# Six recurrent layers on one core: layer 1 made wide, weight loads placed behind gathers, the end split in halves

## What is computed

```python
def reference(r_state, r_token, L0_rec_ih, L0_rec_hh):
    state = r_state                      # 1024 x 256
    for i in range(6):
        gate = ih[i][token]              # 1024 rows of a 4000 x 256 table
        state = tanh(state + (state @ hh[i]) * gate)
    return state
```

## Time and profile before

| | us |
|---|---|
| median of 3 runs | 60.72 (60.33 to 61.02) |
| the profiled execution | 60.63 |
| its span, first to last instruction | 58.8 |
| what lies around the span | 1.83 |
| busy in the span: PE / DVE / ACT / POOL | 51.2 / 39.6 / 39.7 / 35.4 |

### The profile page before, as it was taken

The page is one execution under the profiler, slowest core; times in us unless marked ns, Lnnn a source line. Parts: engine busy times, 40 slices in busy tenths (PEclk is TensorE's granted clock), DMA queues, the critical chain, the costliest instruction groups (busy, mean ns, idle before and its releaser), DMA issues.

```text
span 58.8 us, 869 instructions
## 1 busy us (share of the span) xinstructions
PE 51.2 (87%) x280; PEld 43.9 (75%) x280; DVE 39.6 (67%) x62; ACT 39.7 (68%) x70; POOL 35.4 (60%) x34
## 2 busy tenths in 40 slices
PE   0979999992899999999999999999999999999000
PEld 0769988880868979888888988889888798889000
DVE  1318994974989495485976925999169990799700
ACT  0712899821073449989589999788997889944710
POOL 2076066677408445999963996479953898623400
PEclk9999999999999999999999999999999999999995
DMA  0698978798420000000000000000000000004472
GB/s 0 58 286 252 199 249 277 211 285 269 137 63 0 0 0 11 0 0 0 0 0 0 0 0 0 0 6 0 0 6 0 11 0 0 0 0 178 178 266 91
DMA packets 5524, 4.46 MB, mean 76 GB/s; under 512 B 2202, under 2 KB 5018, under 8 KB 5520
## 3 DMA queue, kind: packets, MB, share of 16 engines
q1 hardware_dynamic: 3312, 3.41, 18.6%
q0 software_dynamic: 1152, 0.73, 5.2%
q10 hardware_dynamic: 1056, 0.27, 2.0%
HBM read 8.92 MB, written 1.05 MB: 169 GB/s over the span
## 4 chain that ended last, share of the span: by engine, by line
PE 65%; DMA 10%; DVE 10%; issue 5%; POOL 2%; ACT 2%; ACTq 1%; DVEq 0%
PE prod L506 23%; PE turned L487 12%; PE prod L460 12%; PE prod L515 12%; DMA gate<-gates_dram,row_of 7%; PE turned L469 6%; DVE gate L368 3%; DMA tok<-token_dram 3%; POOL gate L237 2%; DVE gp L384 2%; DVE gp L437 1%; ACT s L312 1%; DVE pre L389 1%; DVE prod L441 1%; DVE pre L443 1%
## 5 line engine op out<-in xcount | busy, mean ns | idle before, releaser
L253 POOL TENSOR_TENSOR sl<-s,sh 128x512 fp32r<-128x512 f32 x12 | 15.4, 1294 | 6.0 <-ACT s L312 5.8
L506 PE MATMUL prod<-sh,wr 128*128 128x512 f32 (+1 forms) x68 | 17.9, 385 | 0.0
L460 PE MATMUL prod<-w,s 128*128 128x256 f32 x64 | 14.8, 379 | 0.0
L395 DVE TENSOR_TENSOR prod<-prod,gate_t 128x512 f32<-128x512 f32 x14 | 9.8, 700 | 6.6 <-PE prod L515 6.6
L506 PEld LDWEIGHTS prod<-sh,wr 128*128 128x128 f32 x68 | 12.1, 188 | 2.1
L460 PEld LDWEIGHTS prod<-w,s 128*128 128x128 f32 x64 | 11.8, 192 | 1.3
L237 POOL DMA_INDIRECT gate<-gates_dram,row_of x8 | 8.1, 1010 | 5.8 <-issue 2.0
L312 ACT ACTIVATE s<-pre 128x512 f32<-128x512 f32 x15 | 9.3, 623 | 1.1 <-DVE pre L400 1.1
L515 PE MATMUL prod<-sl,wr 128*128 128x512 f32 (+1 forms) x34 | 10.1, 377 | 0.0
L400 DVE TENSOR_TENSOR pre<-prod,s 128x512 f32<-128x512 f32 x14 | 9.7, 692 | 0.5
L297 ACT ACTIVATE s<-pre 128x512 f32<-128x512 f32 x8 | 5.0, 623 | 7.0 <-DVE pre L389 5.7
(11 more groups left out here) (28 smaller groups left out, 32.9 us busy)
## 6 DMA issues: line engine op xcount, KB each, us to landing
w<-hh_dram SPq DMA_DIRECT2D x5, 256.0 KB
s<-state_t_dram SPq DMA_DIRECT2D x4, 256.0 KB, 3.5
out_t_dram<-s SPq DMA_DIRECT2D x3, 256.0 KB, 2.1
w<-hh_dram ACTq DMA_DIRECT2D x1, 256.0 KB
out_t_dram<-s SPq DMA_DIRECT2D x2, 128.0 KB, 2.0
gate<-gates_dram,row_of POOLq DMA_INDIRECT x8, 3.4
last_row<-gates_dram ACTq DMA_DIRECT2D x1, 6.0 KB, 2.7
tok<-token_dram SPq DMA_DIRECT2D x1, 4.0 KB, 1.7
```

The lines of the kernel that those rows point to most:

```text
L253: nc.gpsimd.tensor_tensor(of_unit(sl[:, l % 2], h, c), of_unit(s, h, c), of_unit(sh[:, l % 2], h, c).bitcast(f32), ALU.subtract).then_inc( ...
L395: nc.vector.tensor_tensor(prod_bank[u][:, :], prod_bank[u][:, :], gate_t[:, l % 2, u], ALU.mult).then_inc(unit_gated[u], 1)
L460: last = nc.tensor.matmul(prod[q][:, t, :], of_quarter(s, q)[:, c, t * P:(t + 1) * P], w[:, l, c, :], start=c == 0, stop=c == KC - 1)
L506: nc.tensor.matmul(bank, wr[:, l, k, half, c * P:(c + 1) * P], of_unit(sh[:, (l - 1) % 2], h, k)[:, tokens], start=half == 0 and k == 0, s ...
```

## The change

- WIDE = 1: layer 1 is done in wide units too. Its products are written out in pieces: `rounded` (rounded weights x sh), `low_of_weights`, `low_of_state`; `high_product` is the first two, `low_product` the last. In layers 1 and 2 pieces of several units are interleaved. plain(3) stands behind turn(1), turn(0) in front of plain(2).
- Rounded tanh (sh) now for the quarters of layer 0; ACT's order of tanh, casts and gate copies is new. The remainders sl of quarters 0 and 1 are made by DVE (`low_state`), those of 2 and 3 by POOL.
- SP: state 2 behind state 1, state 3 behind state 2, weights 1 right after; weights 2, 3 and 4 when the gathers of tiles 3, 5 and 7 have landed; weights 5 behind weights 3.
- POOL: `low_weights` 3 to 5 spread among the low states of layers 1 to 3.
- DVE: the last fill stands behind gating(0); patches stand behind gating(1) and gating(2).
- The end: POOL's sum of unit 2 is made in two column halves, with a tanh and a store each.

```diff
-WIDE = 2
+WIDE = 1
+LOAD_BEHIND = {2: 3, 3: 5, 4: 7}
+DVE_LOW = [0, 1]
...
 @block.sync
-                sp.wait_ge(state_in[0], 16)
+                sp.wait_ge(state_in[1], 16)
                 load_state(2)
-                sp.wait_ge(w_in[0], 16)
+                sp.wait_ge(state_in[2], 16)
                 load_state(3)
-                sp.wait_ge(state_in[1], 16)
                 load_weights(1)
-                sp.wait_ge(state_in[2], 16)
-                load_weights(2)
-                sp.wait_ge(state_in[3], 16)
-                load_weights(3)
-                for l in range(4, LAYERS):
-                    sp.wait_ge(w_in[l - 3], 16)
+                for l, t in LOAD_BEHIND.items():
+                    sp.wait_ge(gate_in[t], 16)
                     load_weights(l)
+                sp.wait_ge(w_in[3], 16)
+                load_weights(5)
...
+                sp.wait_ge(unit_s[UNITS - 2], wide_done(LAYERS - 1))
+                store(UNITS - 2, slice(0, QB))
                 sp.wait_ge(unit_s[UNITS - 1], wide_done(LAYERS - 1))
                 store(UNITS - 1, slice(0, QB))
-                sp.wait_ge(unit_s[UNITS - 2], wide_done(LAYERS - 1))
-                store(UNITS - 2, slice(0, HB))
+                sp.wait_ge(late_s, 1)
+                store(UNITS - 2, slice(QB, HB))
...
 @block.gpsimd
-                for l in range(WIDE, LAYERS - 1):
-                    low_weights(l)
-                low_state(0)
-                low_state(1)
-                low_weights(LAYERS - 1)
-                low_state(2)
-                low_state(3)
+                low_weights(1)
+                low_weights(2)
+                for q in range(QUARTERS):
+                    if q not in DVE_LOW:
+                        low_state(q)
                 for l in range(WIDE, LAYERS - 1):
                     for h in range(HALVES):
                         for c in range(KC):
                             wide_low_state(l, h, c)
+                        if (l, h) == (1, 0):
+                            low_weights(3)
+                    if 4 <= l + 2 < LAYERS:
+                        low_weights(l + 2)
...
-                nc.gpsimd.tensor_tensor(of_unit(pre, 1, 0), gated_end, of_unit(s, 1, 0), ALU.add).then_inc(unit_pre[u], 1)
+                nc.gpsimd.tensor_tensor(late_half(pre, 0), gated_end[:, 0:QB], late_half(s, 0), ALU.add).then_inc(unit_pre[u], 1)
+                nc.gpsimd.tensor_tensor(late_half(pre, 1), gated_end[:, QB:HB], late_half(s, 1), ALU.add).then_inc(late_pre, 1)
...
 @block.scalar
+                tanh_rounded(0)
+                tanh(0)
+                round_weights(1)
+                copy_gates(1, 0, 0)
+                tanh_rounded(1)
+                tanh(1)
+                round_weights(2)
+                copy_gates(1, 0, 1)
+                tanh_rounded(2)
+                tanh(2)
+                copy_gates(1, 1, 0)
+                tanh_rounded(3)
+                tanh(3)
+                copy_gates(1, 1, 1)
+                round_weights(3)
+                wide_tanh(1, 0, 0)
+                wide_tanh(1, 0, 1)
+                copy_gates(2, 0, 0)
+                copy_gates(2, 0, 1)
+                wide_tanh(1, 1, 0)
+                wide_tanh(1, 1, 1)
+                copy_gates(2, 1, 0)
+                copy_gates(2, 1, 1)
+                round_weights(4)
+                round_weights(5)
+                for l in range(2, LAYERS - 1):
...
 @block.vector
+                def low_state(q):
+                    dve.wait_ge(s_ready[q], WIDE)
+                    nc.vector.tensor_tensor(of_quarter(sl[:, (WIDE - 1) % 2], q), of_quarter(s, q),
+                                            of_quarter(sh[:, (WIDE - 1) % 2], q).bitcast(f32), ALU.subtract).then_inc(sl_ready[q], 1)
...
                 patch(0, 0, 1)
+                patch(0, 1, 1)
+                gating(0)
                 for i, t, count in DVE_FILLS[3:]:
                     fill(i, t, count)
-                patch(0, 1, 1)
-                gating(0)
-                patch(1, 0, len(EARLY_TILES))
                 sum_up(0)
                 gating(1)
-                patch(2, 0, len(EARLY_TILES))
+                patch(1, 0, len(EARLY_TILES))
                 sum_up(1)
                 gating(2)
-                gating(4)
+                patch(2, 0, len(EARLY_TILES))
+                low_state(0)
                 sum_up(2)
+                low_state(1)
                 gating(3)
-                sum_up(4)
                 sum_up(3)
...
 @block.tensor
                 plain(0)
                 plain(1)
+                turn(0)
                 plain(2)
+                turn_gates(1, 0, 0)
...
                 turn(1)
+                plain(3)
+                turn_gates(1, 0, 1)
+                turn_gates(2, 0, 0)
...
                 turn(2)
+                rounded(1, 0, 0, prod_bank[0][:, :], slice(0, HB))
+                rounded(1, 0, 1, prod_bank[1][:, :], slice(0, HB))
+                low_of_weights(1, 0, 0, prod_bank[0][:, :], slice(0, HB))
+                low_of_weights(1, 0, 1, prod_bank[1][:, :], slice(0, HB))
+                turn_gates(1, 1, 0)
...
                 turn(3)
+                low_product(1, 0, 0)
+                low_product(1, 0, 1)
+                turn_gates(1, 1, 1)
+                turn_gates(2, 0, 1)
+                high_product(1, 1, 0)
+                high_product(1, 1, 1)
+                low_product(1, 1, 0)
+                low_product(1, 1, 1)
+                turn_gates(2, 1, 0)
+                turn_gates(2, 1, 1)
+                wide_product(2, 0, 0)
+                wide_product(2, 0, 1)
+                high_product(2, 1, 0)
+                high_product(2, 1, 1)
+                low_product(2, 1, 0)
+                low_product(2, 1, 1)
+                for l in range(3, LAYERS - 1):
```

More of the change, by code:

```diff
@@ L290, in round_weights, with tanh_rounded, tanh @@
                     nc.scalar.copy(wr[:, l, :, 0], w[:, l]).then_inc(wh_ready, 1)
[L292 to L296, removed]
+                def tanh_rounded(q):
+                    act.wait_ge(pre_ready[q], WIDE)
+                    nc.scalar.activation(of_quarter(sh[:, (WIDE - 1) % 2], q), of_quarter(pre, q), ACT.Tanh).then_inc(sh_ready[q], 1)
+                def tanh(q):
+                    act.wait_ge(pre_ready[q], WIDE)
                     nc.scalar.activation(of_quarter(s, q), of_quarter(pre, q), ACT.Tanh).then_inc(s_ready[q], 1)
@@ L474, in turn_gates @@
                     u = h * KC + c
-                    pe.wait_ge(gated[2 * h], 1)
-                    pe.wait_ge(gated[2 * h + 1], 1)
+                    if l == WIDE:
+                        for t in range(h * TPH, (h + 1) * TPH):
+                            if t not in EARLY_TILES:
+                                pe.wait_ge(gate_in[t], 16)
                     if h == 0:
@@ L491, in wide_product, with high_product, low_product, rounded @@
                 def wide_product(l, h, c):
+                    high_product(l, h, c)
+                    low_product(l, h, c)
+                def high_product(l, h, c):
                     u = h * KC + c
-                    product(l, h, c, prod_bank[u][:, :], slice(0, HB), unit_prod[u])
-                def product(l, h, c, bank, tokens, ready):
-                    pe.wait_ge(wl_ready, l - 1)
+                    rounded(l, h, c, prod_bank[u][:, :], slice(0, HB))
+                    low_of_weights(l, h, c, prod_bank[u][:, :], slice(0, HB))
+                def low_product(l, h, c):
+                    u = h * KC + c
+                    low_of_state(l, h, c, prod_bank[u][:, :], slice(0, HB), unit_prod[u])
+                def rounded(l, h, c, bank, tokens):
                     for k in range(KC):
@@ L518, in product, with end_product @@
                     last.then_inc(ready, 1)
+                def end_product(i, ready):
+                    l, h, c = LAYERS - 1, HALVES - 1, KC - 1
+                    tokens = slice(i * QB, (i + 1) * QB)
+                    rounded(l, h, c, end_bank[i], tokens)
+                    low_of_weights(l, h, c, end_bank[i], tokens)
+                    low_of_state(l, h, c, end_bank[i], tokens, ready)
                 pe.wait_ge(ident_ready, 1)
@@ L533, in _ @@
                 plain(1)
+                turn(0)
                 plain(2)
-                turn(0)
-                plain(3)
+                turn_gates(1, 0, 0)
                 pe.wait_ge(filled_dve, len(DVE_FILLS))
@@ L540, in _ @@
                 turn(1)
-                plain(4)
+                plain(3)
+                turn_gates(1, 0, 1)
+                turn_gates(2, 0, 0)
                 pe.wait_ge(filled_act, len(ACT_FILLS) - 1)
@@ L544, in _ @@
                 turn(2)
-                plain(5)
-                turn(4)
+                rounded(1, 0, 0, prod_bank[0][:, :], slice(0, HB))
[3 more added lines that the diff above has]
+                turn_gates(1, 1, 0)
                 pe.wait_ge(filled_act, len(ACT_FILLS))
```

(16 more changed lines are left out.)

53 lines of the change are left out of this document (25 added, 28 removed).

## The result

The changed kernel takes 61.22 us (median of 4 runs, 61.04 to 61.44), the kernel before 60.52 (4 runs); the ratio is 1.016, interval 1.011 to 1.022. It is slower: by 1.6% by this ratio, by 1.2% by the two medians, and by 0.7% when it was run again (fifth experiment). The forecast was 59.8. The profiled execution of the changed kernel took 61.16 us with a span of 59.3.

A forecast was written before the change was run, and what follows sets the result against it. Bound taken as a head set by the gates' gathers, 38.1 us of PE, and a tail. From 60.63, gains of 0.8 plus 0.15 give 59.7; the median, 0.09 above that execution, makes it 59.8, range 58.8 to 61.0.

The forecast's parts named there:

- When the gates land (T3): Head: tile 3's gather lands and releases gating(1) at 12.9 (bounds 12.5 to 14.0), against 14.00 before.
- low_state(0) 17.2, sum_up(2) 17.8, low_state(1) 18.5, gating(3) 19.1: DVE's queue after gating(1): start times without idle, each low_state taken as 0.63 like a sum.
- Rival 2: DVE's low_state collides with POOL's subtraction, 1.29 us each: 61.1 for one, 62.4 for both; chance 0.1.
- low_state(1) falls where POOL waits for s(2): Argument against the DVE and POOL collision: POOL would be idle, waiting for s(2), when DVE's second low_state runs.
- PE's work: Wide layer 1 takes 1.4 us off PE (8.67 to 7.23), but plain(3), 1.73, now stands behind the wait.
- plus about 1.2 us: If PE never waited, the gain would be the earlier release of gating(1) plus about 1.2 us.
- The stalls for sl: PE waits for POOL's sl at low products of layers 2 and 3: 0.5, 0.15 and 0.2 us lost.
- The tail, 0.15: End of kernel: unit 2's sum, tanh and store in halves gain 0.15 us; bounds 0.7 loss, 0.4 gain.
- Rival 1: Head: gates land as before (tile 3 at 14.0, gating(2) at 16.5), giving 60.9; chance 0.25.

The follow-up runs named there:

- fifth experiment: The changed kernel run again without edits, beside the kernel before on the same chip: 61.23 us, ratio 1.007 (1.000 to 1.015).
- second experiment: The changed kernel with all four low states of layer 0 on POOL, none on DVE: 61.89 us, ratio 1.022 (1.009 to 1.035).
- first experiment: The changed kernel with low_state(1) on DVE moved behind gating(3): 60.40 us, ratio to the kernel before 1.002 (0.996 to 1.007).
- ninth: The changed kernel with low_state(1) behind gating(3) and ACT's tanh pair (2,1,1) in front of layer 3's two gate copies: 60.91 us, ratio 1.003.
- twelfth kernel: The eleventh with states 2, 3 and weights 1 loaded as before, weights 2 to 4 behind gathers of tiles 3, 5, 7: median 61.32 us, ratio 0.985.
- seventh: The changed kernel with SP's load order of the kernel before: 61.53 us, ratio 1.023 (1.014 to 1.031).
- eighth: The changed kernel, both DVE low states behind gating(3), casts moved, plain(3) before turn_gates(1,0,0), states 2, 3 and weights 1 loaded as before: 61.36 us, ratio 1.015.
- tenth: The changed kernel with low_state(1) behind gating(3), old load order, and the kernel before's head order on PE and DVE: 61.81 us, ratio 1.017.
- thirteenth: The twelfth kernel with turn_gates(1,0,0) moved behind turn(1) on PE: 60.90 us (59.67 to 61.25), no ratio that holds.
- sixth: The changed kernel with low_state(1) behind gating(3) and casts of weights 4 and 5 behind the last tanh of layers 2 and 3: 60.81 us, ratio 1.004.
- eleventh: The changed kernel with both the ninth's and the tenth's edits, including the old load order: 61.70 us, ratio 1.016 (1.008 to 1.024).

## Why the prediction was wrong

The profiled execution took 61.16 where its forecast was 59.7. By the stations the 1.46 us are: gating(1) at 13.55 for 13.0, 0.55; from there to layer 3's gate turns 19.35 for 18.7 (31.7 less 13.0), 0.65; layer 3 to 4 7.51 for 7.45, 0.06; from there to the end of the span 18.9 for 18.72 (59.7 less 1.83 less 39.15), 0.17; around the span 0.03. Two steps failed: the landing of tile 3, and DVE's order up to gating(3).

- *"When the gates land (T3) ... I take 12.9".* This step failed. It carried more than the whole gain: the forecast had layer 4's gate turns 26.15 us behind gating(1) (39.15 less 13.0), which is 0.28 more than the kernel before (25.87). All that was forecast beyond that came from T3 1.1 us earlier. The runs have 3.1 to 4.0 us from issue to release with the new order and 3.4 to 4.2 with the old one. I had read one execution's 4.0 us as the effect of loads beside it, and bounded below by tile 0 at 2.6. What the loads held is tile 1 (its patch at 9.36 to 10.03 where states 2, 3 and weights 1 were loaded as before, at 7.93 to 8.62 with the new order), whose work ends inside the wait for tile 3 all the same.
- *"low_state(0) 17.2, sum_up(2) 17.8, low_state(1) 18.5, gating(3) 19.1", with 0.63 for each.* This failed too. The second took 1.20, so gating(3) came 6.52 behind gating(1) in place of 6.1. Rival 2 stood for this, with the right mechanism (one waits the other out) and its sign came true (a low_state over 1 us), but at a chance of 0.1. Its price, 1.29 for each, was paid in no run: where DVE's started within 0.1 us of POOL's, DVE's took 0.66 to 0.69 and POOL's was the one held (1.75 to 1.87), and low_state(1) met the last 0.65 us and lost 0.51. "low_state(1) falls where POOL waits for s(2)" was wrong because low_weights(2) started only 0.05 us behind low_state(0) and waited 0.50 for it, and so was still running. What POOL pays the second experiment shows: low_weights(2) takes 1.29 without a DVE subtraction beside it, in the changed kernel 1.79.
- *Order.* The larger fault was not the collision but what stands behind it: 0.76 us came back by letting gating(3) pass low_state(1), which nothing needed so early. I had priced the subtraction in the chain and didn't ask whether it had to be there. With it moved, the kernel has 18.59 and 26.10 behind gating(1), close to the forecast's 18.7 and 26.15, which had the subtraction in place at its small price; that closeness is luck. Even so it would be no faster than the kernel before, and its ratio is 1.002.
- *PE's work.* The text saw that plain(3) behind the wait (1.73) takes back the cut of 1.44, and then let T3 decide. Its "plus about 1.2 us" is a wrong sum: it counts the 0.93 from the release to turn(1) for the kernel before alone, though the changed one has it too (13.46 to 14.38, 0.92), and four gate turns (1.75) where three (1.31) stand behind the wait. Put right, PE's own work falls by 1.44 - 1.73 + 0.44 = 0.15. The first experiment has 18.59 to layer 3, the kernel before 18.63. That plain(3) back in the wait would bring more isn't shown: the versions with it there have 18.56 to 19.86.
- *The stalls for sl.* Forecast 0.5, 0.15 and 0.2; the last, at the low product of (3,1,0), is the 0.27 of layer 3, caused by two gate copies in front of a tanh pair (ninth).
- *The tail, 0.15.* ACT's halves came as worked out (POOL 0.73 each by the trace), but the end of the span didn't follow: from layer 4's gate turns to it 18.9 us (59.3 - 40.41), before 18.8 (58.8 - 39.97). Nothing is won.
- *Rival 1* (gates as before) had the right cause for its part and gave 60.9; it and a shortened collision of rival 2 came together, and I had treated them as exclusive.

## What to carry to other kernels

A gain that rests on a transfer landing earlier needs its landing time from several executions, not one; here one profile's half microsecond was scatter, and the whole forecast hung on it. When work for another engine's later need is put in a queue, put it behind the instruction that the chain waits for: one place on DVE was worth 0.76 us up to layer 3. Two subtractions on DVE and POOL that both read SBUF twice took turns here (POOL's 1.79 for 1.29, then DVE's 1.20 for 0.69), so a short one can pass its delay on to the next. When PE's work is cut, look at what was running in a wait for free; moving 1.73 us of it behind the wait cancels a cut of 1.44 (worked out from the rows, not shown by a version that gained by moving it back).

## What the runs showed of the hardware that was not expected

First, PE ran at half its pace (0.43 us a matmul for 0.22) for a while in the head of some executions, and the granted clock of the page doesn't show it. The twelfth kernel, first matmuls of its head, and the first windows:

```profile
6.49 3.84 PE L491 MATMUL prod<-w,s 128*128 128x256 f32 x9
...
9.48 2.15 PE L491 MATMUL prod<-w,s 128*128 128x256 f32 x8
```
```profile
6.00:8.00 2.00, 2.00 (x8) 1.73 (x7) 2.00 (x4) 1.73 (x4) 0.00 (x0) 1.00 0.81 213
8.00:10.00 2.00, 2.00 (x6) 1.55 (x6) 1.83 (x3) 2.00 (x4) 1.59 (x2) 1.00 0.75 230
10.00:12.00 2.00, 2.00 (x11) 1.77 (x10) 1.61 (x3) 1.97 (x3) 1.38 (x2) 1.00 0.26 75
```

The windows say clock 1.00 throughout, but only 6 to 8 matmuls touch the two windows until 10 (the 8 with short transposes among them), and 11 the one after. Eight plain matmuls cost 0.43 us each, the later ones 0.22 (1.73 for eight in the earlier trace rows). That is a factor of two; what makes it, the clock or something else, isn't shown. PE had been busy without a break since 3.88, after 0.76 us without work behind its warm-up. The ninth kernel was also late, sixteen matmuls in 5.15 us where the changed kernel took 4.06:

```profile
6.40 5.15 PE L490 MATMUL prod<-w,s 128*128 128x256 f32 x16
```
```profile
6.16 4.06 PE L487 MATMUL prod<-w,s 128*128 128x256 f32 x16
```

Yet the ninth took 60.23 us: with one plain quarter less in front of gating(1) it has slack there, while the twelfth, with plain(3) in the wait, passed the delay on. Whether this slow stretch also explains the spread of the execution times isn't shown, since only one execution of each kernel has a trace.

Second, a DVE and a POOL subtraction that both have two inputs in SBUF took turns in these traces. A DVE one that starts 0.15 to 0.65 us in front of the end of POOL's ends 0.54 or 0.55 us behind it, in nine of nine cases (changed kernel, fifth, seventh, eighth, tenth to twelfth, and two in the thirteenth), whether that makes it 0.70 or 1.20 long; one that starts in the last 0.06 us takes 0.67 to 0.69 (first, sixth, ninth). A POOL one that starts within 0.1 us of DVE's takes 1.75 to 1.87 in place of 1.29 (changed kernel, first, fifth, sixth, seventh, ninth). DVE's gatings and sums, with one input in PSUM, take 0.67 to 0.70 beside POOL (in the changed kernel 0.69 at 18.35).

Third, turn(1)'s signal is held 1.4 and 0.8 us behind its matmuls in the tenth and eleventh kernels. Both have the full old load order and nothing that PE can run behind turn(1). Of three other traces with the old order, and of two (eighth and twelfth) with the same order behind turn(1) and mixed loads, none has the hold. No instruction in the trace explains it; its cause stays open.
